# Second attention to the context: keys and values per batch on chip, scores once by query, sums by ACT, rounding by POOL

## The reference

```python
def _dyn_quant(x):
    s = jnp.maximum(jnp.max(jnp.abs(x), axis=-1, keepdims=True) / 127.0, EPS)
    q = jnp.clip(jnp.round(x / s), -127.0, 127.0)
    return (q, s)
...
def _w8a8_linear(x, w, b):
    qx, sx = _dyn_quant(x)
    qw, sw = _quant_weight(w)
    y = jnp.einsum('bnc,oc->bno', qx, qw) * (sx * sw[:, 0])
    return y + b
...
q = _w8a8_linear(x, wq, bq).reshape(B, N, H, D).transpose(0, 2, 1, 3)
k = (cond @ wk.T + bk).reshape(B, L, H, D).transpose(0, 2, 1, 3)
v = (cond @ wv.T + bv).reshape(B, L, H, D).transpose(0, 2, 1, 3)
scores = jnp.einsum('bhnd,bhld->bhnl', q, k) * inv_sqrt_d + mask[:, None]
attn = jax.nn.softmax(scores, axis=-1)
o = jnp.einsum('bhnl,bhld->bhnd', attn, v)
o = o.transpose(0, 2, 1, 3).reshape(B, N, C)
return _w8a8_linear(o, wo, bo)
```

## Time and profile before

| what | us |
|---|---|
| median of three runs (2838.26 to 2840.66) | 2840.01 |
| profiled execution, its own time | 2836.32 |
| its span | 2834.5 |
| PE busy in the span | 2405.4 |
| DVE, ACT, POOL busy | 1236.4, 855.3, 709.5 |

### The profile page before, as it was taken

The page is one execution under the profiler, slowest core; times in us unless marked ns, Lnnn a source line. Parts: engine busy times, 40 slices in busy tenths (PEclk is TensorE's granted clock), DMA queues, the critical chain, the costliest instruction groups (busy, mean ns, idle before and its releaser), DMA issues. The chain is left out here.

```text
span 2834.5 us, 37569 instructions
## 1 busy us (share of the span) xinstructions
PE 2405.4 (85%) x14496; PEld 1879.0 (66%) x14496; DVE 1236.4 (44%) x2784; ACT 855.3 (30%) x1295; POOL 709.5 (25%) x667
## 2 busy tenths in 40 slices
PE   6999999999975888789999996678777855999974
PEld 4989889889864666678887775555453644555542
DVE  2343443343454553531111233465555455567535
ACT  2222222222222434322111112344444222444332
POOL 2532332231302532024333001433332010121210
PEclk8999999999986978899999998797788976999986
DMA  4000000000006652101000000321220645534101
GB/s 175 20 8 12 27 19 9 12 19 9 1 1 135 130 107 55 49 30 53 15 30 0 1 1 27 53 45 32 40 47 16 212 119 110 120 89 94 44 8 60
DMA packets 91967, 144.10 MB, mean 51 GB/s; under 512 B 10864, under 2 KB 64752, under 8 KB 88816
## 3 DMA queue, kind: packets, MB, share of 16 engines
q1 hardware_dynamic: 91792, 141.71, 20.5%
HBM read 82.95 MB, written 17.30 MB: 35 GB/s over the span
## 5 line engine op out<-in xcount | busy, mean ns | idle before, releaser
L1183 PE MATMUL PS<-WH,bXH 128*128 128x512 f32 x512 | 201.6, 394 | 5.4 <-POOL WL L1460 5.4
L1183 PE MATMUL PS<-WL,bXH 128*128 128x512 f32 x512 | 200.8, 392 | 0.0
L1183 PE MATMUL PS<-WH,bXL 128*128 128x512 f32 x512 | 200.8, 392 | 0.0
L558 DVE TENSOR_TENSOR xN<-PS,xN 128x512 f32<-128x512 f32 x128 | 88.5, 692 | 227.7 <-PE PS L361 227.7
L1852 DVE TENSOR_REDUCE aM<-PS 128x4 f32<-128x1024 f32 x128 | 153.1, 1219 | 67.0 <-PE PS L1694 66.3
L1378 DVE SCALAR_TENSOR_TENSOR s<-s,cf,PS 128x256 f32<-128x256 f32 x112 | 53.9, 481 | 250.2 <-ACT s L1298 241.2
L330 PE MATMUL PS<-aXH,QKH 128*128 128x512 f32 x384 | 152.3, 397 | 0.0
L330 PE MATMUL PS<-aXH,QKL 128*128 128x512 f32 x384 | 149.6, 390 | 0.0
L330 PE MATMUL PS<-aXL,QKH 128*128 128x512 f32 x384 | 149.6, 389 | 0.0
L1798 ACT ACTIVATE aPT<-PS 128x1024 f32<-128x1024 f32 x128 | 128.7, 1025 | 68.2 <-PE PS L1714 67.7
L643 POOL TENSOR_TENSOR E<-E,DM 128x256 f32<-128x256 f32 x64 | 47.1, 736 | 392.5 <-ACT E L475 392.5
(11 more groups left out here) (429 smaller groups left out, 6383.6 us busy)
## 6 DMA issues: line engine op xcount, KB each, us to landing
ckr<-in_cS SPq DMA_DIRECT2D x48, 256.0 KB, 7.1
cqs<-cQH SPq DMA_DIRECT2D x64, 128.0 KB, 3.8
sg<-in_gu SPq DMA_DIRECT2D x8, 1024.0 KB, 5.0
aqs<-aQH SPq DMA_DIRECT2D x64, 128.0 KB, 4.0
xks<-zkH SPq DMA_DIRECT2D x16, 512.0 KB, 8.2
xqs<-xQH SPq DMA_DIRECT2D x64, 128.0 KB, 2.6
gQK<-in_Wqk SPq DMA_DIRECT2D x8, 768.0 KB, 4.3
V<-in_xT SPq DMA_DIRECT2D x4, 1024.0 KB, 6.0
```

The lines of the kernel that those rows point to most:

```text
L558: e.tensor_tensor(xN[:, t, :], PS[:, b, :], xN[:, t, :], ALU.add).then_inc(o_add.sem, 1)
L1183: mm = e.matmul(PS[:, b, :], x[:, kc, 128 * t:128 * t + 128], w[:, kc, :], start=kc == 0 and i == 0, stop=kc == KC - 1 and i == 2)
```

## The change

`cross1_keys`, `Quant` and `Cross1` go, and `cross1` does it all, from a table of its own. What is different:

- Keys and values of one batch are projected on chip (12 products of 128x256 for each of 4 key tiles, 12 of 128x512 for each of 2 value tiles) and stay there. The context and the mask are loaded for each batch.
- The 8 weight pieces are rounded before the table starts.
- Scores are made once, by query, four heads in four row tiles of 32 partitions, 24 products to a group of four heads (`scores`). All groups use the same four PSUM banks, 0 to 3, so a group waits for the exponentials of the one before. Queries carry a factor of -1/sqrt(32), the mask is negated by POOL, and DVE takes a minimum (`soft`).
- ACT takes exponentials of 128x256 with the minimum as bias and writes the row sums itself (`accum_out`), 32 a batch. PE turns them (`flip`, 64 transposes of 128x128 a batch), ACT copies them, `pv` makes 8 products for a group of four heads and none for the sums.
- Rounding of x and of the attention's result is POOL's, two instructions of two operations for each tile; DVE only makes the scale. The turns are of f32, and ACT removes the rounding constant on the copy.
- SP's mask load of `context` j waits for all minima of batch j - 2.

The table puts into the 8 slots of a period, here of batch j, with j+1 and j+2 for later batches and "prev" for the one before: (0) soft 0, flip 7 prev, key 3 and turn j+1; (1) soft 1, flip 0, value 0 j+1, pv 3 prev, scores 1; (2) soft 2, flip 1, project 0 j+1, fin prev; (3) soft 3, flip 2, value 1 and project 1 j+1, pv 0, round_o prev, scores 2; (4) soft 4, flip 3, context j+2; (5) soft 5, flip 4, key 0 and round 0 j+2, pv 1, turn_o prev, scores 3; (6) soft 6, flip 5, key 1 and round 1 j+2, out 0 prev; (7) soft 7, flip 6, key 2 j+2, pv 2, out 1 prev, scores 0 j+1. The norms n1 to n4 stand in slots 2 to 5 of every second period.

POOL before, one batch of the second stage: a split of queries and of the mask, and the adds of two output tiles (`xoN` is the attention's result, `xN` the rows of x, `boB` the bias).

The minima of soft 1 stand behind the copy, which waits for PE's scale. The diff, cut:

```diff
-class Quant:
...
-def cross1_keys(K):
...
-    plan = plan_of(J, lambda j: ["round0", "round1", "turn", "project", "scale"], range(8), 1,
-                   ((1, "den"), (2, "fin"), (3, "round_o"), (5, "turn_o"), (6, "out"), (8, "n1"), (9, "n2"), (10, "n3"),
-                    (10, "n4")), 17)
...
+def cross1(K):
...
+    for j in range(J):
+        base = 8 * j
+        put(base - 12, 3, "context", j)
+        for i in range(4):
+            put(base - 11 + i, 4, "key", j, i)
+        for i in (0, 1):
+            put(base - 7 + 2 * i, 4, "value", j, i)
+        put(base - 11, 5, "round", j, 0)
+        put(base - 10, 5, "round", j, 1)
+        put(base - 8, 5, "turn", j)
+        put(base - 6, 5, "project", j, 0)
+        put(base - 5, 5, "project", j, 1)
+        for g in range(4):
+            put(base + 2 * g - 1, 9, "scores", j, g)
+            put(base + 2 * g, 1, "soft", j, 2 * g)
+            put(base + 2 * g + 1, 1, "soft", j, 2 * g + 1)
+            put(base + 2 * g + 1, 2, "flip", j, 2 * g)
+            put(base + 2 * g + 2, 2, "flip", j, 2 * g + 1)
+            put(base + 2 * g + 3, 6, "pv", j, g)
+        put(base + 10, 8, "fin", j, 0)
+        put(base + 10, 8, "fin", j, 1)
+        put(base + 11, 7, "round_o", j, 0)
+        put(base + 11, 7, "round_o", j, 1)
+        put(base + 13, 7, "turn_o", j)
+        put(base + 14, 7, "out", j, 0)
+        put(base + 15, 7, "out", j, 1)
+        if j % 2 and j < 7:
+            for i, what in enumerate(("n1", "n2", "n3", "n4")):
+                put(base + 18 + i, 8, what, j)
+    plan = [what for slot in sorted(at) for _, _, what in sorted(at[slot], key=lambda x: x[:2])]
...
+    R.take("scores", 4)
...
+            elif what == "turn":
+                for a in (0, 1):
+                    b, left = rooms["turn", j, a]
+                    for w in left:
+                        e.wait_ge(*w)
+                    e.wait_ge(*r_rnd.upto(nth["q", j, a]))
+                    for c in range(KC):
+                        mm = e.transpose(PS[:, b, 128 * c:128 * c + 128], qr[a][:, 128 * c:128 * c + 128], idF[:, :])
+                    mm.then_inc(q_turn.sem, 1)
+                b, left = rooms["scale", j]
+                for w in left:
+                    e.wait_ge(*w)
+                e.wait_ge(*s_dg.upto(2 * j + 6))
+                for a in (0, 1):
+                    mm = e.matmul(PS[:, b, 128 * a:128 * a + 128], K.onesF[:, :], dg[:, a, :], start=True, stop=True,
+                                  skip_group_check=True)
+                mm.then_inc(s_mm.sem, 1)
...
+            elif what == "scores":
+                n = 4 * j + i
+                if i == 0:
+                    e.wait_ge(*k_lo.upto(4 * j + 4))
+                    e.wait_ge(*k_hi.upto(4 * j + 4))
+                    e.wait_ge(*q_lo.upto(2 * j + 2))
+                    e.wait_ge(*q_hi.upto(2 * j + 2))
+                if n:
+                    e.wait_ge(*s_exp.upto(2 * n))
+                for q in (0, 1):
+                    for k, (w, x) in enumerate(pair3((QH[y], KH[y]), (QL[y], KL[y]))):
+                        for r in range(4):
+                            mm = e.matmul(PS[:, r, 256 * q:256 * q + 256],
+                                          w[32 * r:32 * r + 32, i, 128 * q:128 * q + 128], x[32 * r:32 * r + 32, i, :],
+                                          start=q == 0 and k == 0, stop=k == 2, skip_group_check=True)
+                mm.then_inc(s_in.sem, 1)
+            elif what == "flip":
+                b, left = rooms["flip", j, i]
+                for w in left:
+                    e.wait_ge(*w)
+                e.wait_ge(*s_exp.upto(8 * j + i + 1))
+                for a in (0, 1):
+                    h = 2 * (i % 2) + a
+                    for q in (0, 1):
+                        for kt in (0, 1):
+                            mm = e.transpose(PS[:, b + a, 256 * kt + 128 * q:256 * kt + 128 * q + 128],
+                                             P[(i // 2) % 2][:, h, q, 128 * kt:128 * kt + 128], idF[:, :])
+                mm.then_inc(f_in.sem, 1)
+            elif what == "pv":
+                b, left = rooms["pv", j, i]
+                for w in left:
+                    e.wait_ge(*w)
+                e.wait_ge(*f_out.upto(8 * j + 2 * i + 2))
+                e.wait_ge(*v_out.upto(2 * j + 2))
+                for kt in (0, 1):
+                    for r in range(4):
+                        h = 4 * i + r
+                        mm = e.matmul(PS[32 * r:32 * r + 32, b, 0:256], V[y][:, kt, 32 * h:32 * h + 32],
+                                      PT[i % 2][:, r, kt, :], start=kt == 0, stop=kt == 1)
+                mm.then_inc(a_mm.sem, 1)
...
+            elif what == "soft":
+                n = 8 * j + i
...
+                    e.wait_ge(*n_rec.upto(j - 1))
+                for a in (0, 1):
+                    h, r = 2 * i + a, 2 * (i % 2) + a
+                    e.wait_ge(*s_max.upto(2 * n + a + 1))
+                    for q in (0, 1):
+                        last = e.activation(P[(i // 2) % 2][:, r, q, :], PS[:, r, 256 * q:256 * q + 256], ACTF.Exp,
+                                            bias=M[y][:, q, h:h + 1], scale=-1.0, accum_out=den[y][:, q, h, :])
+                last.then_inc(s_exp.sem, 1)
...
+        def scale_of(src, s, r):
+            step(e.tensor_reduce(s, src, AX.X, ALU.max, apply_absolute_value=True))
+            step(e.tensor_scalar(s, s, float(np.float32(1.0) / np.float32(127.0)), 1e-8, ALU.mult, ALU.max))
+            return e.reciprocal(r, s)
...
+            elif what == "turn":
+                if j == 0:
+                    e.wait_ge(*s_mm.upto(1))
+                else:
+                    e.wait_ge(*p_dq.upto(2 * j))
+                for a in (0, 1):
+                    e.tensor_scalar(dg[:, a, :], idF[:, :], sx[:, a:a + 1], None, ALU.mult).then_inc(s_dg.sem, 1)
+                e.wait_ge(*s_mm.upto(j + 2))
+                e.tensor_copy(sxB[:, :], PS[:, rooms["scale", j][0], 0:256]).then_inc(s_out.sem, 1)
+                e.wait_ge(*s_out.upto(j + 2))
...
+                e.wait_ge(*s_in.upto(4 * j + i // 2 + 1))
+                for a in (0, 1):
+                    h, r = 2 * i + a, 2 * (i % 2) + a
+                    for q in (0, 1):
+                        s = PS[:, r, 256 * q:256 * q + 256]
+                        last = e.tensor_tensor_reduce(out=s, in0=s, in1=mk[y][:, q, :], scale=1.0, scalar=3.0e38,
+                                                      op0=ALU.add, op1=ALU.min, accum_out=M[y][:, q, h:h + 1])
+                    last.then_inc(s_max.sem, 1)
...
+        def rounded(key, src, n, buf):
+            e.tensor_scalar(buf[:, :], src, sr[:, n:n + 1], 127.0, ALU.mult, ALU.min).then_inc(r_min.sem, 1)
+            e.wait_ge(*r_min.upto(nth[key]))
+            e.tensor_scalar(buf[:, :], buf[:, :], -127.0, MAGIC, ALU.max, ALU.add).then_inc(r_rnd.sem, 1)
...
+            if what == "context":
+                e.wait_ge(*x_hi.upto(j + 1))
+                e.tensor_tensor(XL[:, :, :], cst[y][:, :, :], XH[:, :, :].bitcast(F32), ALU.subtract).then_inc(x_lo.sem, 1)
+                e.wait_ge(*in_mk[y].upto(j // 2 + 1))
+                e.tensor_scalar(mk[y][:, :, :], mk[y][:, :, :], -1.0, None, ALU.mult).then_inc(mk_neg.sem, 1)
+            elif what == "round":
+                if j:
+                    e.wait_ge(*q_turn.upto(2 * j - 1 + i))
+                elif i == 0:
+                    e.wait_ge(*w_mm.upto(8))
+                    e.wait_ge(*in_b.upto(4))
+                e.wait_ge(*r_max.upto(2 * j + i + 1))
+                rounded(("q", j, i), xN[:, 2 * j + i, :], i, qr[i])
+                e.wait_ge(*r_min.upto(nth["q", j, i]))
+                e.tensor_tensor(xN[:, 2 * j + i, :], xN[:, 2 * j + i, :], boB[:, :], ALU.add).then_inc(r_bias.sem, 1)
...
+            if what == "context":
+                if j >= 2:
+                    e.wait_ge(*s_max.upto(16 * j - 16))
+                e.dma_start(mk[y][:, :, :], d["mask"][:, 2 * j:2 * j + 2, :]).then_inc(in_mk[y].sem, 16)
...
```

More of the change, by code:

```diff
@@ new lines, in cross1 @@
+        if what == "key":
+            R.use(("k", j, i), 1, k_lo.upto(4 * j + i + 1))
+        elif what == "value":
+            R.use(("v", j, i), 1, v_out.upto(2 * j + i + 1))
+        elif what == "turn":
+            for a in (0, 1):
+                R.use(("turn", j, a), 1, q_turned.upto(2 * j + a + 1))
+            R.use(("scale", j), 1, s_out.upto(j + 2))
+        elif what == "project":
+            R.use(("project", j, i), 1, p_dq.upto(2 * j + i + 1))
+        elif what == "flip":
+            R.use(("flip", j, i), 2, f_out.upto(8 * j + i + 1))
+        elif what == "pv":
+            R.use(("pv", j, i), 1, a_out.upto(4 * j + i + 1))
@@ L2337, in cross1 @@
         elif what == "fin":
-            R.take(("f1", j), 1, pack=True)
-            R.take(("f2", j), 2)
-            R.give(("f1", j), 1, f_rec.upto(j + 1))
-            R.give(("f2", j), 2, f_out.upto(j + 1))
```

(24 more changed lines are left out.)

877 lines of the change are left out of this document (294 added, 583 removed).

## The result

The median of four runs is 2889.80 us (2888.87 to 2892.47) against 2840.34 before: a ratio of 1.0176, interval 1.0158 to 1.0194. I forecast 2855, slower. The sign and the range hold, the size does not: 49 us instead of 15.

What follows compares the result with a forecast made beforehand. PE bound the old batches; the new one was taken as a chain round PE, DVE, ACT and POOL. Four quarters sum to 62.2 us a period against 41.7, the stage ends 16 later, so 2855 us, range 2815 to 2895.

Steps and rivals of the forecast that it cites:

- second quarter: Maxima 2 and 3 of a batch: DVE and ACT pass work back and forth, 15.4 us.
- first quarter: Maxima 0 and 1: mask load, POOL's negation and query roundings, then PE up to scores 1, 18.6 us.
- third quarter: Maxima 4 and 5: POOL's output roundings and context split, then PE's key 0 to scores 3, 15.7 us.
- last quarter: Maxima 6 and 7: exponentials, key high half, DVE's work to the last minimum, and 4.1 more, 12.45 us.
- seventh batch: The batch that loads and rounds nothing, put at 50 us against 62.2 for a full period.
- last batch and tail: Last batch, shorter still at 36 us, and its tail as before but with POOL's rounding, 20.5 us.
- The same again to 13.15: Second quarter: the DVE and ACT exchange that ends with a minimum at 8.9 us repeats, ending at 13.15.
- The head: Stage start: all 8 weight pieces rounded first, PE's first key at 2228, first minimum near 2264.
- full clock: Rival: PE is back at 2.4 GHz at once, 3.7 us less a period, 2825 us, faster; chance 0.27.
- Heads in line: Rival: four heads' score products run one after another, 45 us more in seven periods, 2900 us; chance 0.08.
- dear exponentials: Rival: ACT's exponentials cost 0.63 us each instead of 0.50, 15 us more in seven periods, 2870 us; chance 0.08.
- DVE's stalls beside POOL: Rival: two DVE instructions a period each wait out a POOL instruction, 28 us in seven, 2883 us; chance 0.14.

Runs made afterwards that it cites:

- the unread products: The changed kernel plus 24 and 20 matmuls a batch that nobody reads, before two waits of PE: 2866.68 us, ratio 1.0104.
- the same work in another order: The changed kernel with mask negation, keys, project 1, first context's high half, and output turn and products moved: 2771.62 us, ratio 0.9772.

## Why the prediction was right in sign and wrong in size

The steps that failed are two terms of the sum, the second quarter at 15.4 and the third at 15.7. They measured 18.5 and 18.1, because PE's order, its banks and a reused buffer put steps on the path that I had left out. Over five batches that is 27 of the 39 us by which the stage's end missed: forecast at 2745, it came at 2784.2. The 39 us, term by term, from the starts of DVE's minima:

| term | forecast | measured | difference |
|---|---|---|---|
| stage's start | 2199.6 | 2204.8 | 5.2 |
| from there to the first minimum | 64.4 | 67.8 | 3.4 |
| first batch | 49.5 | 51.2 | 1.7 |
| first quarter, five batches | 18.6 each | 17.3 to 19.6 | -1 |
| second quarter, without the norm | 15.4 | 18.5 | 15.5 |
| third quarter, without the norm | 15.7 | 18.1 | 11.8 |
| last quarter | 12.45 | 12.2 to 13.7 | 1.8 |
| norms | 14 | 11.4 | -2.6 |
| seventh batch | 50 | 55.1 | 5.1 |
| last batch and tail | 56.5 | 55.1 | -1.4 |

The stage's start is no step of the prediction. In the seventh batch 3.3 of the 5.1 are the second quarter again (18.7 for the 15.4 of the other batches); the rest stays open.

**Right.** The wait for the mask, behind which POOL's roundings stand (first quarter, to 1 us over five; a move of that one instruction gave 31 to 42 us), POOL's roundings (2.0 and 1.93 against 1.93), the load (3.0 assumed, the negation starts 2.8 to 3.7 after the last minimum), the minima (steps of 0.38), four heads side by side, exponentials at 0.45 between 0.43 and 0.63. Groups of the kernel after (busy us, mean ns of one, idle before):

```profile
L2478 POOL TENSOR_SCALAR qtmp<-qtmp 128x512 f32<-128x512 f32 x32 | 61.7, 1928 | 2.6
...
L2315 ACT ACTIVATE xP<-PS,xM 128x256 f32<-128x256 f32 x256 | 117.9, 477 | 134.2 <-DVE xM L2429 126.2 <-PE PS L2218 7.9
...
L2429 DVE CUSTOM_DVE_ANT_0 PS<-PS,xmk 128x256 f32<-128x256 f32 x256 | 100.3, 455 | 16.2 <-PE PS L2205 15.6 <-POOL xmk L2486 0.2
```

**Wrong, the second quarter.** "The same again to 13.15" let DVE and ACT set the pace and had PE's project 1 ready. It was not. In the timeline of a later batch (kernel after), a flip starts only when the first quotient has ended, which frees its bank, and value 1, whose first four products step by 0.38 to 0.57 where the later ones step by 0.23, stands ahead of project 1 (granted clock 0.68 from this flip to project 1):

```profile
2559.60 1.29 DVE L2442 TENSOR_TENSOR xoN<-PS,xrc 128x512 f32<-128x512 f32 x2
...
2560.39 1.94 PE L2218 MATMUL PS<-idF,xP 128*128 128x128 f32 x8 [2.15 <-issue]
...
2561.99 0.78 PE L2160 MATMUL PS<-xWVH,xXH 128*128 128x512 f32 x1
...
2565.61 1.05 PE L2189 MATMUL PS<-qxT,qw 128*128 128x256 bf16 x8
```

The flip's row names no releaser; that it waits for the bank is read from the kernel's order and from the times. I had costed each engine's steps in the quarter, but not PE's order among them, nor its banks. With project 1 first the quarter fell by 1.2 to 3.6, to 16.3 on the mean without the norm; the 0.9 that are left over my 15.4 I have not taken apart.

**Wrong, the third quarter.** The PE line was priced right (6.5 from the split to the end of scores 3; in the timeline above 2440.1 to 2446.6), but I ended the quarter there. The wait of key 0's high half on the buffer that scores 3 reads puts 0.5 of ACT, 0.5 of DVE and a 1.0 scale behind it. The other 0.6 is POOL, whose split ends 9.8 after the quarter's start, where I had 9.2.

**The head, nearly right.** PE's first key comes 29.2 after the stage's start, where I had 28.4. I had let the context's split lie beside the weights; on ACT it stands behind them, 2.4 of waiting for PE. The stalls of DVE came out cheaper than the 5 us that I gave (one of 3.6). The 2.6 between the first key and the first minimum I did not take apart.

**The rivals.** The full clock fell: 0.63 to 0.84 in the quarters of the batch above, and the unread products took 18.7 us off six periods, 3.1 a period, where I had allowed 3.7 for the half clock. Heads in line fell (six rounds of products in 0.9 us), dear exponentials fell. DVE's stalls beside POOL fell as a cost of the batches, where the minima kept their step. They are real in the head, as above, and off the path in the batches: diagonals of the scales took up to 1.36 while POOL was at work, instead of 0.28, 2.7 us in all from the second batch on, but DVE then waits for PE's scale all the same (36.8 us in six waits). The Trainium skill ("SBUF — State Buffer", Who interferes with whom) says that a tensor_scalar may take the ports that DVE shares with GpSimd and then one fully blocks the other, while an instruction with at most one SBUF input outside the two-port modes is free. The trace agrees with both halves: 4.13 and 4.31 instead of 0.49, and minima in steps of 0.38, those from 2430.25 on beside POOL's roundings from 2429.49 on too.

## What to carry to other kernels

When an engine that works in order gets a step that waits for something late, everything behind it in its list waits too; look up what that is, and on which engine the next one stands still for it. In a ring that no engine fills, work it out to the end of the last step of each engine, buffers and PSUM banks included, since a reused buffer puts a step behind its reader. The gain of doing less was there: the same work in another order took 118 us less.

## What the runs showed of the hardware that I had not expected

More products made the kernel faster: 44 unread ones a batch raised the granted clock of two quarters by 0.19 and 0.18 and took 17.7 us off the stage (23 between the medians). Four heads' 24 products of 32 rows took 0.9 us in all, no more than eight products of 256 columns at 0.119 would. ACT's written row sum took 0.19 to 0.21 us by its rows but only 0.02 a piece in the line: exponentials with it step by 0.45, the plain instruction of the same shape by 0.43. Two exponentials of the kernel after, and the row sum between them:

```profile
2387.43 0.47 ACT L2315 ACTIVATE xP<-PS,xM 128x256 f32<-128x256 f32 x1 [3.00 <-DVE xM L2429]
2387.80 0.19 ACT L2315 ACTIVATION_READ_ACCUMULATOR xP<-PS,xM 128x1 f32 x1
2387.89 0.46 ACT L2315 ACTIVATE xP<-PS,xM 128x256 f32<-128x256 f32 x1
```
